# A change of order around the boundary between token groups: values matmuls, last states of the scan, one decay and one load

## What is computed

```python
x = x + _L0_xattn_ref(_layernorm(x), ctx_1024, ctx_1024, Wq, bq, Wk, bk, Wv, bv)
x = x + _L0_attn_ref(_layernorm(x), x_proj_w, dt_proj_w, dt_proj_b, A_log, D, B_proj_w, C_proj_w, conv_w, conv_b, out_proj_w)
x = x + _L0_ffn_ref(_layernorm(x), gate_weight, e_bias, gate_proj, up_proj, down_proj)
```

## Time and profile before

| | |
|---|---|
| median of three runs | 1280.95 us |
| the profiled execution | 1277.22 us, of which 1275.3 us are the span of the core |
| TensorE (PE) busy | 1112.0 us, 87% of the span |
| VectorE (DVE) busy | 895.9 us, 70% |
| ScalarE (ACT) busy | 623.4 us, 49% |
| mean granted TensorE clock | 0.943 |
| chain that ended last | PE 55%, DVE 28%, ACT 7%, DMA 5%, issue 3% |

### The profile page before, as it was taken

One profiled execution on the slowest core, in us unless ns is written; L12 is line 12 of the kernel. 1 busy time (PEld: TensorE's weight loads), 2 busy tenths in 40 slices (PEclk: granted clock), 3 DMA queues, 4 the chain that ended last, 5 costly groups with the idle time before them and its releaser, 6 DMA issues.

```text
span 1275.3 us, 13226 instructions
## 1 busy us (share of the span) xinstructions
PE 1112.0 (87%) x4228; PEld 710.1 (56%) x4228; DVE 895.9 (70%) x960; ACT 623.4 (49%) x1378; POOL 134.1 (11%) x113
## 2 busy tenths in 40 slices
PE   5997869998988999989899997439999999899992
PEld 4885646765745676665477674325554445454451
DVE  1312589998879999878999996569999966133312
ACT  4552676663667565476656546324455413222230
POOL 0001110001000250000052000130000001033002
PEclk9997989999989999989999999569999999999996
DMA  8368656877600364400144140089999967999994
GB/s 293 117 213 301 213 214 206 255 239 258 231 8 18 116 181 112 153 9 18 51 146 135 50 150 1 33 260 340 371 372 356 368 257 243 382 372 407 410 360 132
DMA packets 115187, 266.25 MB, mean 209 GB/s; under 512 B 11280, under 2 KB 44208, under 8 KB 115120
## 3 DMA queue, kind: packets, MB, share of 16 engines
q1 hardware_dynamic: 99248, 207.22, 47.7%
q0 software_dynamic: 15872, 58.20, 12.1%
HBM read 197.07 MB, written 68.32 MB: 208 GB/s over the span
## 4 chain that ended last, share of the span: by engine, by line
PE 55%; DVE 28%; ACT 7%; DMA 5%; issue 3%; POOL 1%; SPq 1%; POOLq 0%; ACTq 0%; DVEq 0%
PE bank L819 11%; DVE state L1370 10%; PE bank L687 7%; PE bank L699 6%; PE bank L720 6%; PE bank L840 6%; PE bank L780 6%; DVE state L1367 5%; PE bank L798 4%; DVE decay L1374 3%; PE bank L751 3%; ACT decay L1118 2%; DMA bc_bcast<-bc_scratch 2%; DMA queries_ctx<-in_xp_t 2%; PE bank L809 2%
## 5 line engine op out<-in xcount | busy, mean ns | idle before, releaser
L1370 DVE TENSOR_TENSOR_SCAN state<-decay,state 128x2048 f32<-128x2048 f32 x64 | 283.0, 4421 | 12.1 <-ACT decay L1118 11.2
L819 PE MATMUL bank<-expert_w,block_x_t 128*128 128x512 f32 x496 | 226.3, 599 | 2.2 <-ACT block_x_t L1172 2.2
L687 PE MATMUL bank<-decay,params 128*128 128x512 f32 x360 | 165.6, 605 | 6.3 <-DVE decay L1374 6.3
L1673 POOL DMA_INDIRECT dispatched<-ffn_x,slot x32 | 74.1, 2315 | 669.8 <-DVE slot L1474 661.2
L819 PEld LDWEIGHTS bank<-expert_w,block_x_t 128*128 128x128 f32 x496 | 91.4, 195 | 93.5 <-issue 90.7
L1118 ACT ACTIVATE decay<-delta_even,params 128x256 f32<-128x256 f32 x256 | 107.2, 499 | 59.1 <-PE bank L687 56.8
L720 PE MATMUL bank<-probs,ctx 128*128 128x256 f32 x512 | 121.3, 392 | 7.5 <-ACT probs L1015 7.5
L1529 DVE SCALAR_TENSOR_TENSOR hidden<-hidden,bank 128x256 f32<-128x256 f32 x62 | 26.1, 421 | 137.6 <-ACT hidden L1176 131.5
L1118 ACT ACTIVATE decay<-delta_odd,params 128x256 f32<-128x256 f32 x256 | 106.2, 499 | 30.5 <-PE bank L687 27.1
L840 PE MATMUL bank<-expert_w,hidden_t 128*128 128x512 f32 x248 | 116.9, 594 | 2.9 <-ACT hidden_t L1186 2.9
L780 PE MATMUL bank<-normed_t,queries_ctx 128*128 128x256 f32 x512 | 115.0, 385 | 4.6 <-ACT u_odd L1051 1.9
(11 more groups left out here) (192 smaller groups left out, 1327.5 us busy)
## 6 DMA issues: line engine op xcount, KB each, us to landing
dispatched<-ffn_x POOLq DMA_DIRECT2D x38, 1024.0 KB, 6.0
expert_w<-in_eg_t SPq DMA_DIRECT2D x62, 512.0 KB
expert_w<-in_eu_t SPq DMA_DIRECT2D x62, 512.0 KB
expert_w<-in_ed_t SPq DMA_DIRECT2D x62, 512.0 KB
ctx<-in_ctx_t SPq DMA_DIRECT2D x32, 512.0 KB, 7.2
ctx<-in_ctx_n SPq DMA_DIRECT2D x32, 512.0 KB, 3.8
bc_bcast<-bc_scratch SPq DMA_DIRECT2D x64, 256.0 KB, 6.1
block_x<-dispatched SPq DMA_DIRECT2D x62, 256.0 KB
```

The lines of the kernel that those rows point to most:

```text
L687: mm = pe.matmul(y_bank[c][:, :], ident, dA[(g * NS + j) % NDEC][:, c * 512:(c + 1) * 512], start=(j == 0), stop=(j == NS - 1))
L819: mm = pe.matmul(o, xbT[q % 2][:, c, :], w_gu[q % NW][:, :, c, :], start=(c == 0), stop=(c == DC - 1))
L1370: dve.tensor_tensor_scan(h, dA[n % NDEC][:, 0:sw], h, 0.0, ALU.mult, ALU.add).then_inc(scan_rd, 1)
L1673: pool.indirect_dma_start(xd[WAVE_OF[c]], bass.IndirectOffsetOnAxis(slot[:, i:i + 1].bitcast(U32), 0), fx[:, t, :], None).then_inc(dispatc ...
```

## The change

It moves work and removes none: the same instructions are issued in another order. In TensorE the sum of the last unit's state goes behind the values and the transposes, and the sum of state 13 goes behind the projections. In ScalarE the decay of state 14 goes behind the standard deviation. In VectorE the part 2 of state 13 goes behind the norm, and the parts of state 15 each go one piece of the convolution later. In SyncE's queue the rows of state 15 go behind the projection weights.

```diff
@@ sync
-                for s in range(NS - TAIL, NS):
-                    load_bc(g * NS + s)
+                load_bc(g * NS + NS - 2)
                 load_proj(g + 1)
+                load_bc(g * NS + NS - 1)
                 store_bc(g + 1)
@@ tensor, attention
                 weighted_ctx(UNIT0[g] + NUS[g] - 1)
-                if g > 0:
-                    for s in unit_states(g - 1, NUS[g] - 1):
-                        sum_state(g - 1, s)
...
                 if g > 0:
-                    for s in range(NS - TAIL - PRE, NS - PRE):
+                    for s in unit_states(g - 1, NUS[g] - 1) + list(range(NS - TAIL - PRE, NS - PRE - 1)):
                         sum_state(g - 1, s)
@@ tensor, projections
                 if g > 0:
-                    for s in range(NS - PRE, NS):
+                    for s in range(NS - PRE - 1, NS):
                         sum_state(g - 1, s)
@@ scalar, projections
                 norm_std(NTS[g])
+                if g > 0:
+                    scan_decay(g - 1, NS - TAIL)
                 norm_copy(xT[g], NTS[g])
@@ scalar, main loop
                 attention_units(g + 1)
-                scan_decay(g, NS - TAIL)
                 attn_end(g + 1)
@@ vector, main loop
                 late = list(range(NS - TAIL - 2, NS))
-                for s in range(TAIL):
-                    scan_step(g, late.pop(0))
+                scan_step(g, late.pop(0))
+                scan_step(g, late[0], parts=(0, 1))
                 add_tiles(g + 1)
...
-                for s in range(PRE - 1):
-                    scan_step(g, late.pop(0))
-                for k in range(0, NBK, 2):
-                    if k // 2 in range(SCAN_PARTS - 1):
-                        scan_step(g, late[0], parts=(k // 2,))
-                    conv(g + 1, k)
+                scan_step(g, late.pop(0), parts=(2,))
+                scan_step(g, late.pop(0))
+                conv(g + 1, 0)
+                scan_step(g, late[0], parts=(0,))
+                conv(g + 1, 2)
+                scan_step(g, late[0], parts=(1,))
+                conv(g + 1, 4)
+                scan_step(g, late[0], parts=(2,))
+                conv(g + 1, 6)
                 join_states(g)
```

## The result

The changed kernel takes 1269.07 us in the median of 17 runs (1263.36 to 1274.87); the kernel before takes 1282.96 us beside it (17 runs, 1275.36 to 1290.23). The ratio is 0.9885, 95% interval 0.9868 to 0.9901: **1.15% faster**. The prediction was 1270.6 us, in a range of 1267 to 1276.5. The profiled execution took 1268.13 us, against 1277.22 before.

What follows compares the result with a forecast made beforehand. The bound was taken to be a chain through TensorE at the three boundaries, with the sum of state 11 on it. 5.3 + 5.3 - 0.2 = 10.4 us off the median 1280.95 gave 1270.6 us, range 1267 to 1276.5.

Steps and rivals of the forecast that it cites:

- B: Second of the three boundaries: 2.57 us lead at the read-out plus 2.75 us from the clock, gain 5.3 us.
- The front: TensorE's values ahead of the sum of state 11: they start 0.73 us behind the last product, 2.71 us earlier.
- C: Third boundary: same front, but its read-out starts the moment the sums are over; claimed a loss of 0.2 us.
- The norm and the moved decay: ScalarE's table load and decay of 14, now behind the square root, hold the norm's copies; lead shrinks to 2.26 us.
- Rival (e): Drain behind the moved table load: norm's copies 1.38 us later, 1.38 less in A and B, 1273.3; chance 0.02.
- The projections: TensorE's 128 matmuls lose both stops, 0.69 and 0.27 us, so their end moves 3.22 us earlier.
- The back: Two sums behind the projections hold ScalarE's read-out, lead 2.57 us; output projection at full clock gives 2.75 us more.
- rival (a): Clock falls again ahead of the output projection, taking back up to 2.4 + 2.75 us, 1275.7 us; chance 0.2.
- rival (b): Rows of state 15 land late for VectorE's scan: about 3 us less gain, 1273.5 us; chance 0.12.
- A: First boundary: lead 3.0 us at the read-out, 2.4 us from the output projection, 0.1 charged; gain 5.3 us.
- (c): Sum of 13 behind the projections costs more than the front gives: 4.2 us slower, 1285.2 us; chance 0.06.
- (d): No change: the front gives about 1.4 us a boundary, or VectorE takes all, 1281 us; chance 0.07.

Runs made afterwards that it cites:

- Experiment 1: Changed kernel with the sum of the last unit's state ahead of the values again and the decay of 14 ahead of their copies: 1278.3 us, ratio 0.9940 to before.
- experiment 8: Changed kernel with the parts of state 15 ahead of the first three pieces of the convolution, as before: 1279.26 us, ratio 0.9956 to the kernel before.
- experiment 6: Changed kernel with C's read-out of the sums moved behind the logarithm, as in A and B: 1261.38 us, ratio 0.9813 to the kernel before.
- Experiment 4: Changed kernel with state 13 whole ahead of the norm and its sum ahead of the norm's transposes: 1276.01 us, ratio 0.9914 to the kernel before.
- experiments 7 and 10: Useless matmuls ahead of the last product with the context: four on the changed kernel, 1269.94 us; two on the kernel of experiment 6, 1259.05 us.
- experiment 6 again: Repeat of experiment 6, the changed kernel with C's read-out behind the logarithm: 1262.39 us, ratio 0.9817 to the kernel before.

## Why the prediction was right, step by step

In what follows a place is counted from the start of the last product with the context, in B, and a lead is how much sooner than before the place is reached.

**The front.** Predicted: values 0.73 us behind the product, 2.71 sooner. Measured: 0.69, and 6.10 us in place of 8.77, 2.67 sooner; the add of the attention 15.81 in place of 18.62, 2.81 sooner. Right. Experiment 1 takes it out and pays 2.1 us in B and, at like clock, 2.3 in C. The wait on VectorE is 1.84 us and not as long as before (2.34), so the split off product did clear the way.

**The norm and the moved decay.** Predicted lead 2.26 us at the norm's copies; measured 26.29 against 23.85, 2.44. The decay's wait for the sum of 11 did not bind. The table load took 1.28 us and the exponential began 0.02 behind it. The Trainium skill, page ScalarE: Activation LUTs, section "What ACT_TABLE_LOAD costs", counts a drain of about 1.38 us with every switch; this trace doesn't agree, at a place that had not been a switch before. Rival (e) is out.

**The projections.** Predicted: both stops go, 0.96 us. They went, and the 128 matmuls shrank from 29.39 to 27.89 us, by 1.50. This term was under-sized by 0.54 us: the matmuls themselves, 28.4 us busy in three rows, take 27.9 in one. The prediction had 3.55 us a job of 16, a third of a row of 10.63; the difference of the rows of 48 and 32 matmuls, 10.63 - 7.17, gives 3.46 a job, so each row holds some 0.25 us besides its matmuls, and each stop adds that to the idle time that it shows. Lead at the end of the projections: 3.97 us, against 3.22 predicted.

**The back.** Predicted: the two sums hold the read-out by some 0.65 us. Measured: ScalarE's wait for the bank is 0.53. Lead at the read-out 3.35 us (61.60 for 64.95) against 2.57; the wait ahead of the output projection 1.28 us against 1.1; the projection 14.00 us against 13.97. B gained 6.04 in place of 5.3, and the excess is, within 0.03, that of the lead at the end of the projections, 0.75 us: 0.54 for the stops and 0.21 for their start, 2.47 us sooner where the sum had 2.26.

**The clock, rival (a).** It was given 0.2; no run with this order bears it out. Over all profiles of the study the output projection took 16.40 to 17.03 us in the four cases behind a wait of 4.06 or 4.11 us, and 13.90 to 14.00 us in all 24 behind 1.33 us or less. Between, behind C's 2.15 us, it took 14.0 us in six cases and 15.7 in eight. The new wait of 1.3 us has room.

**Rows of state 15, rival (b).** It was given 0.12, and it is out by very little. The rows' issue in A, in the view by tile of the changed kernel:

```profile
L422 SPq DMA_DIRECT2D bc_bcast<-bc_scratch x1: 366/366/366, 310.2 to 310.2; - x1
...
DMA to landing us min/median/max: 11.8/11.8/11.8
```

Issued at 310.2 and landed 11.8 us later, at 322.0; VectorE's part 0 starts at 322.04 with no wait. The prediction had them landing 1.6 to 2.6 us behind the need (324.6 and one or two, against 324.0), and charged 0.1 for what follows. The need was right, since A stands 2.0 us sooner in this profile; the dt weights landed 17.6 us behind their issue and not 18.6, and the rows 0.6 us behind them and not one or two. The rows landed behind the weights, as it said, but added next to nothing of their own. Had VectorE been sooner it would have waited: it does so, 2.85 us, in experiment 8. A gained 5.8 in place of 5.3, mostly for the same reason as B.

**C** gained 0.5 in place of losing 0.2: the same 0.7 us. The sums do hold the read-out, 3.85 us of wait, as the prediction said; that this was a price that could be avoided by one line (experiment 6, 5.9 us) it did not see. It took the order of the read-out in C as given.

**Slower or no change, rivals (c) and (d).** They were to decide at a front lead of 1.4 us a boundary; the lead was 2.8 at the add and 4.0 at the end of the projections. Experiment 4, with the third sum at the front, shows the other side of the trade: the back gets its second sum off, and loses 2.9 to 3.1 us to the clock.

**The sum.** 10.4 us predicted, 12.4 measured in the boundaries. It was off by 0.5 to 0.7 us three times over, most of it the idle time of two stops taken for their whole cost. The prediction also had it that what a boundary gains stays gained, and that holds only in part: in the pair of profiles 3.3 of the 12.4 us are lost outside the boundaries, 1.4 of them between B and C in rows that are slowed with the changed order. And that 1270.6 lies 1.5 us from 1269.07 is in part luck: by the medians the gain was 13.9 us, 3.5 more than forecast, and it was taken from 1282.96 us and not from 1280.95, so that two misses offset one another.

## What to carry to other kernels

Where an engine waits just ahead of a long run of matmuls, compare the length of the run with its length at full clock: if it is longer, shortening the wait, or filling it with useless matmuls that end before the data come, wins on top of the wait, while a filling that overruns gives all back. The edits of an order by hand have their price together: with one product moved behind the norm, the old order of the queue costs 33 us and the old place of the convolution 9, in part because the waits that they open bring the clock down too. After such a change look again at every instruction that was placed by the old timing, as C's read-out was, which was worth half of what the whole change brought.

## What the runs showed of the hardware

- A wait of 1.8 to 2.3 us ahead of the last product: in 28 of 36 cases the product was slowed, 5.2 to 5.4 us in place of 3.7, and in 8 it was not; without the wait (experiments 7 and 10) in none of six. The order of the instructions doesn't decide it: A's product took 5.41 us in experiment 6 and 3.72 in its repeat, behind the same wait of 2.32. At such waits the clock falls in some executions and not in others, and some of the spread from run to run is there. The windows of the last product, at 0.72 in B of the changed kernel and at 1.00 in A of experiment 6 again:

```profile
494.20:500.30 6.10, 5.41 (x16) 4.09 (x16) 6.03 (x3) 1.20 (x2) 0.00 (x0) 0.72 0.20 42
```

```profile
287.87:292.20 4.33, 3.72 (x16) 2.96 (x16) 4.29 (x2) 1.17 (x2) 0.72 (x1) 1.00 0.79 243
```

- Waits ahead of or inside the 128 rows of the projections, in A, B and C of the 14 profiles: behind the eight from 2.54 us up (to 12.72) the rows were slowed, by 1.6 to 3.0 us (a mean clock of 0.78 behind the 3.30 us of experiment 8), and behind those up to 2.08 they never were.
- A small load behind two large ones waits for them: 256 KB took 11.8 us in A behind 4096 KB on one queue, where it took 6.6 in the median of before; the second of the large ones took 17.6 us, and the small one, issued 6.4 us after it, landed 0.6 us behind it. Its time there was that of its place in the queue and not of its size.
- The wait for the x weights in A varied from 0 to 4.9 us between kernels that have the same loads, beside POOL's transfers of 1024 KB. It was no part of the change, and it is why A alone can't weigh an edit.
